# Layer 0's token routing: from a stage of its own into the last steps of the first attention

## What is computed

```python
xn = layernorm(x)
x  = x + attention(xn) + conditional(xn)
# conditional: 2 sequences of 1024 in the formula's default, here 8 of 256
s      = einsum("bnd,rd->brn", xn, routing_token)[:, 0]
a, b   = 0, -s
repeat 50 times:
    a  = log(k_eff) - logsumexp(s + b);  b = -relu(s + a)
scores = exp(s + a + b)
sel, idx = top_k(scores, num_tokens)      # 128 query tokens; 256 key tokens = all of them
light  = windowed attention over all tokens (8 heads)
heavy  = attention of the chosen tokens (8 heads) with a null key
out    = light + (heavy at idx, null_q elsewhere)
```

## Time and profile before

| | |
|---|---|
| median of 3 runs | 1793.24 us (1793.17, 1793.24, 1802.02) |
| the profiled execution | 1782.04 us, span 1780.20 us, mean granted TensorE clock 0.953 |
| busy: PE / DVE / ACT / POOL | 1575.2 / 1183.5 / 1002.4 / 375.5 us |
| first attention | 59.14 to 361.91 |
| routing stage | 361.91 to 384.14 |
| second attention | from 384.14 |

### The profile page before, as it was taken

The page is one execution under the profiler, slowest core; times in us unless marked ns, Lnnn a source line. Parts: engine busy times, 40 slices in busy tenths (PEclk is TensorE's granted clock), DMA queues, the critical chain, the costliest instruction groups (busy, mean ns, idle before and its releaser), DMA issues. The chain is left out here.

```text
span 1780.2 us, 31999 instructions
## 1 busy us (share of the span) xinstructions
PE 1575.2 (88%) x10960; PEld 1094.2 (61%) x10960; DVE 1183.5 (66%) x3106; ACT 1002.4 (56%) x2683; POOL 375.5 (21%) x386
## 2 busy tenths in 40 slices
PE   4799999959999999899999989588989957899986
PEld 2577777726666666567778766355556733555653
DVE  5599998747777777646545434577743358999964
ACT  2488887706666666444454434133453427888845
POOL 0100000000000000010122015332452410888830
PEclk8899999979999999989999999799999978999998
DMA  4000000040000000110000011400012130233200
GB/s 141 1 1 1 1 1 1 1 141 1 1 1 1 1 1 1 55 57 1 13 16 16 25 31 64 165 1 1 15 36 62 46 90 14 88 86 89 86 21 24
DMA packets 43980, 62.50 MB, mean 35 GB/s; under 512 B 7576, under 2 KB 29920, under 8 KB 43008
## 3 DMA queue, kind: packets, MB, share of 16 engines
q1 hardware_dynamic: 39280, 51.08, 9.6%
q0 software_dynamic: 4544, 9.38, 1.5%
HBM read 49.88 MB, written 15.75 MB: 37 GB/s over the span
## 5 line engine op out<-in xcount | busy, mean ns | idle before, releaser
L591 ACT ACTIVATE probs<-psum_all,pair_negmax 128x256 f32<-128x256 f32 x512 | 235.8, 473 | 158.9 <-DVE pair_negmax L690 86.7
L2116 POOL TENSOR_TENSOR weighted<-state,c_all 128x512 f32<-128x512 f32 x128 | 163.6, 1298 | 77.5 <-DVE state L2126 62.5
L690 DVE TENSOR_REDUCE pair_negmax<-psum_all 128x2 f32<-128x512 f32 x192 | 123.6, 685 | 66.9 <-PE psum_all L506 66.9
L2126 DVE TENSOR_TENSOR_SCAN state<-decay,psum_all 128x512 f32<-128x512 f32 x128 | 148.9, 1199 | 15.4 <-PE psum_all L2044 12.5
L716 DVE TENSOR_SCALAR probs<-probs,pair_recip 128x256 f32<-128x256 f32 x512 | 146.1, 349 | 4.5
L506 PE MATMUL psum_all<-keys,queryT 64*128 64x256 f32 x1024 | 143.9, 400 | 2.8 <-ACT probs L591 2.7
L602 ACT ACTIVATE probsT<-psum_all 128x512 f32<-128x512 f32 x256 | 140.0, 611 | 0.7 <-PE psum_all L517 0.5
L531 PE MATMUL psum_all<-probsT,values 128*64 128x256 f32 x1024 | 138.8, 392 | 0.0
L517 PE MATMUL psum_all<-ident,probs 128*128 128x128 f32 x1024 | 133.1, 273 | 2.8 <-ACT probsT L602 1.9
L517 PEld LDWEIGHTS psum_all<-ident,probs 128*128 128x128 f32 x1024 | 119.1, 141 | 18.1 <-issue 4.4
L506 PEld LDWEIGHTS psum_all<-keys,queryT 64*128 64x128 f32 x1024 | 92.6, 189 | 54.6 <-issue 46.6
(11 more groups left out here) (369 smaller groups left out, 3281.4 us busy)
## 6 DMA issues: line engine op xcount, KB each, us to landing
c_all<-c_rows SPq DMA_DIRECT2D x64, 256.0 KB, 3.3
slots<-slot_fill_dram SPq DMA_DIRECT2D x2, 2535.0 KB, 14.6
ring<-slots SPq DMA_DIRECT2D x18, 260.0 KB, 3.0
keys<-found SPq DMA_DIRECT2D x16, 256.0 KB, 4.7
up<-up_dram SPq DMA_DIRECT2D x1, 2048.0 KB, 7.8
down<-down_dram SPq DMA_DIRECT2D x1, 2048.0 KB, 12.3
up<-up_dram SPq DMA_DIRECT2D x1, 1408.0 KB, 6.1
found<-values,dest POOLq DMA_INDIRECT x78, 2.2
```

What stands on the lines that cost most here:

```text
L591: nc.scalar.activation(k.probs[:, 2 * (u % PAIR_BUF) + j, t, :], k.psum[score_bank(u, j)][:, SEQ * t:SEQ * (t + 1)], ACT.Exp, bias=k.pair_ ...
L690: nc.vector.reduce_max(k.pair_negmax[:, u % 2, SUB * j:SUB * (j + 1)], src, AXX, negate=True).then_inc(s.negmax_ready, 1)
L2116: nc.gpsimd.tensor_tensor(w.weighted[:, u % RING, :], w.state[:, u % RING, :], w.c_all[:, u // L3_DC % C_RING, :], ALU.mult)\
L2126: nc.vector.tensor_tensor_scan(w.state[:, u % RING, :], w.decay[:, u % L3_RING, :, :].rearrange("p b n -> p (b n)"), k.psum[u % PARTS_RING ...
```

## The change

`route_stage` goes, and with it one border between stages and the unread product of `keep_running` in it. Its operations move into the first attention:

- step 49: VectorE subtracts and clips the scores at its end, ScalarE makes the exponential; SP sends the scores and reads them back spread;
- step 50: VectorE makes the weights;
- step 51: the four transposes are a job of TensorE, `route_turn`, in bank 7 behind the values job of the last sequence, and VectorE saves it;
- steps 53 to 62: one rank pair at the end of each, on VectorE; steps 64, 65 and 66: two each;
- step 67: the choice, behind the last `add_output`.

The spread scores land in the upper half of `keys`, which the first attention doesn't use, since `probs` is in use there. Each rank pair now waits for the one before it, and all write the same two buffers; before, two pairs could be under way. The second attention gets the five new semaphores too but doesn't use them.

```diff
@@ -364,6 +364,8 @@
 PAIR_BUF, PAIR_TBUF = 3, 2
 PBUF = 4
 SEQS = BATCH
+ROUTE = Names(scores=DESCENT_STEPS + 1, exp=DESCENT_STEPS + 1, weights=DESCENT_STEPS + 2, turn=DESCENT_STEPS + 3,
+              ranks={DESCENT_STEPS + 5 + n: (n,) for n in range(10)} | {SEQS * PAIRS + i: (10 + 2 * i, 11 + 2 * i) for i in range(3)}, choice=SEQS * PAIRS + 3)
 
 
@@ -379,6 +381,8 @@
             (before if q == 0 else late[PAIRS * q - 5 + i]).append(job)
         if ffn:
             late[PAIRS * (q + 1) + 1].append(("null_probs", q, 0))
+    if not ffn:
+        late[ROUTE.turn].append(("route_turn", 0, 0))
     return before, early, late
 
...
-                 "output_made", "output_added", "route_dve", "route_act", "act_step", "dve_step") as s:
+                 "output_made", "output_added", "route_dve", "route_act", "act_step", "dve_step", "scored", "exped", "weighted", "sent", "spread") as s:
 
         def wait_saved(engine, job):
@@ -460,6 +464,12 @@
                     sp.dma_start(slots, k.dram["slot_fill"]).then_inc(s.filled, 16)
                 if fills:
                     sp.wait_ge(s.filled, 16 * len(fills))
+                if not ffn:
+                    sp.wait_ge(s.scored, 1)
+                    sp.dma_start(k.scratch, k.logits[0:BATCH, :]).then_inc(s.sent, 16)
+                    sp.wait_ge(s.sent, 16)
+                    sp.dma_start(c.w.scores_all[:, :, :].rearrange("p b n -> p (b n)"),
+                                 k.scratch.rearrange("b n -> (b n)").partition_broadcast(P)).then_inc(s.spread, 16)
 
             @block.tensor
@@ -485,6 +495,12 @@
                     elif what == "null_scores":
                         for t in range(SUB):
                             last = nc.tensor.matmul(jb[:, PAIRS * t:PAIRS * (t + 1)], xb[:, 1, P * t:P * (t + 1)], c.w.null_w[:, :], start=True, stop=True)
+                    elif what == "route_turn":
+                        pe.wait_ge(s.scored, 1)
+                        pe.wait_ge(s.weighted, 1)
+                        for a, rows in enumerate((k.logits, k.route_arg)):
+                            for t in range(SUB):
+                                last = nc.tensor.transpose(jb[:, 16 * (SUB * a + t):16 * (SUB * a + t + 1)], rows[:, P * t:P * (t + 1)], k.ident[0:16, 0:16])
                     elif what == "null_probs":
                         pe.wait_ge(s.null_weights, PAIRS // 2 * (q + 1))
@@ -624,6 +640,9 @@
                         save_out(u - V_AFTER)
                     if not ffn and u < DESCENT_STEPS:
                         descend(u)
+                    if not ffn and u == ROUTE.exp:
+                        act.wait_ge(s.scored, 1)
+                        nc.scalar.activation(k.route_exp[:, :], k.logits[:, :], ACT.Exp).then_inc(s.exped, 1)
                     for job in early[u] + late[u]:
                         do(job)
+                    elif what == "route_turn":
+                        ins = nc.vector.tensor_copy(k.route_cols[:, :, :, :].rearrange("p a t r -> p (a t r)"), jb[:, 0:4 * 16])
                     elif what == "values":
                         ins = nc.vector.tensor_copy(k.values[:, q % 2, :, 0:HD], jb[:, 0:SUB * HD].rearrange("p (t n) -> p t n", t=SUB))
@@ -745,83 +766,62 @@
                         normalise(u - 1)
                     for job in late[u]:
                         do(job)
-                    if not ffn and u <= DESCENT_STEPS:
...
+                    if ffn:
+                        continue
+                    if u <= DESCENT_STEPS:
                         descend(u)
-
-
-def route_stage(nc, k, w):
-
-
-    with signals(nc, "dve_step", "scored", "exped", "weighted", "sent", "spread", "turned", "cols_saved") as s:
-        with nc.Block() as block:
-            @block.vector
-            def _(dve):
-                step = Steps(dve, s.dve_step)
-                step.add(nc.vector.tensor_scalar(k.logits[:, :], k.logits[:, :], k.neg_a[:, :], 0.0, ALU.subtract, ALU.min))
-                step.wait()
-
-                nc.vector.tensor_scalar(k.logits[:, :], k.logits[:, :], -103.0, None, ALU.max).then_inc(s.scored, 1)
-                dve.wait_ge(s.exped, 1)
-                step.add(nc.vector.tensor_scalar(k.route_arg[:, :], k.route_exp[:, :], -1.0, 1.0, ALU.mult, ALU.add))
-                step.wait()
-                nc.vector.tensor_tensor(k.route_arg[:, :], k.route_arg[:, :], k.route_exp[:, :], ALU.add).then_inc(s.weighted, 1)
-                dve.wait_ge(s.turned, 1)
-
-                nc.vector.tensor_copy(k.route_cols[:, :, :, :].rearrange("p a t r -> p (a t r)"), k.psum[0][:, 0:4 * 16]).then_inc(s.cols_saved, 1)
-                dve.wait_ge(s.cols_saved, 1)
-                dve.wait_ge(s.spread, 16)
-                n = 0
-                for b in range(BATCH):
-                    for t in range(SUB):
-                        mine = k.route_cols[:, 0, t, b:b + 1]
-                        i = SUB * b + t
-                        if n >= 2:
-                            dve.wait_ge(s.dve_step, step.n - 2)
-                        step.add(nc.vector.tensor_scalar(w.compare[:, n % 2, :], w.scores_all[:, b, :], mine, 0.0, ALU.is_gt, ALU.add,
-                                                         accum_out=k.rank[:, 0, i:i + 1]))
-                        step.add(nc.vector.scalar_tensor_tensor(w.compare[:, 2 + n % 2, :], w.scores_all[:, b, :], mine, w.earlier[:, t, :],
-                                                                ALU.is_equal, ALU.mult, accum_out=k.rank[:, 1, i:i + 1]))
-                        n += 1
-                step.wait()
-                step.add(nc.vector.tensor_tensor(k.rank[:, 0, :], k.rank[:, 0, :], k.rank[:, 1, :], ALU.add))
-                step.wait()
-                selected = k.route_w[:, 0, :]
-                step.add(nc.vector.tensor_scalar(selected, k.rank[:, 0, :], float(NQ), None, ALU.is_lt))
-                step.add(nc.vector.tensor_scalar(k.route_w[:, 1, :], k.rank[:, 0, :], float(NQ), None, ALU.is_ge))
-                step.wait()
-                by_token = k.route_cols[:, 1, :, :].rearrange("p t r -> p r t")
-                step.add(nc.vector.tensor_tensor(selected.rearrange("p (b t) -> p b t", t=SUB), selected.rearrange("p (b t) -> p b t", t=SUB),
-                                                 by_token[:, 0:BATCH, :], ALU.mult))
-                step.add(nc.vector.tensor_copy(k.route_w[:, 2, :].rearrange("p (b t) -> p b t", t=SUB), by_token[:, BATCH:2 * BATCH, :]))
-
-            @block.scalar
-            def _(act):
-                act.wait_ge(s.scored, 1)
-                nc.scalar.activation(k.route_exp[:, :], k.logits[:, :], ACT.Exp).then_inc(s.exped, 1)
-
-            @block.sync
-            def _(sp):
-
-                sp.wait_ge(s.scored, 1)
-                sp.dma_start(k.scratch, k.logits[0:BATCH, :]).then_inc(s.sent, 16)
-                sp.wait_ge(s.sent, 16)
-                sp.dma_start(w.scores_all[:, :, :].rearrange("p b n -> p (b n)"),
-                             k.scratch.rearrange("b n -> (b n)").partition_broadcast(P)).then_inc(s.spread, 16)
-
-            @block.tensor
-            def _(pe):
-                pe.wait_ge(s.scored, 1)
-                for t in range(SUB):
-                    nc.tensor.transpose(k.psum[0][:, 16 * t:16 * (t + 1)], k.logits[:, P * t:P * (t + 1)], k.ident[0:16, 0:16])
-                pe.wait_ge(s.weighted, 1)
-                for t in range(SUB):
-                    last = nc.tensor.transpose(k.psum[0][:, 16 * (SUB + t):16 * (SUB + t + 1)], k.route_arg[:, P * t:P * (t + 1)],
-                                               k.ident[0:16, 0:16])
-                last.then_inc(s.turned, 1)
-                pe.wait_ge(s.dve_step, 2 + 2 * TILES - 14)
-                keep_running(nc, k, 7, 5)
-
-
+                    if u == ROUTE.scores:
+                        route_scores(nc, k, s, step)
+                    if u == ROUTE.weights:
+                        route_weights(nc, k, s, step)
+                    if u == DESCENT_STEPS + 5:
+                        wait_saved(dve, ("route_turn", 0, 0))
+                        dve.wait_ge(s.spread, 16)
+                    for m in ROUTE.ranks.get(u, ()):
+                        route_rank(nc, k, c.w, step, m)
+                    if u == ROUTE.choice:
+                        route_choice(nc, k, step)
+
+
+def route_scores(nc, k, s, step):
+
+    step.wait()
+    step.add(nc.vector.tensor_scalar(k.logits[:, :], k.logits[:, :], k.neg_a[:, :], 0.0, ALU.subtract, ALU.min))
+    step.wait()
+    nc.vector.tensor_scalar(k.logits[:, :], k.logits[:, :], -103.0, None, ALU.max).then_inc(s.scored, 1)
+
+
+def route_weights(nc, k, s, step):
+
+    nc.vector.wait_ge(s.exped, 1)
+    step.add(nc.vector.tensor_scalar(k.route_arg[:, :], k.route_exp[:, :], -1.0, 1.0, ALU.mult, ALU.add))
+    step.wait()
+    nc.vector.tensor_tensor(k.route_arg[:, :], k.route_arg[:, :], k.route_exp[:, :], ALU.add).then_inc(s.weighted, 1)
+
+
+def route_rank(nc, k, w, step, n):
+
```

(24 more changed lines are left out.)

2 lines of the change are left out of this document (1 added, 1 removed).

## The result

| | before | changed |
|---|---|---|
| median, 6 runs each | 1793.28 us (1789.81 to 1802.02) | 1778.05 us (1769.58 to 1780.15) |
| profiled execution, span | 1782.04, 1780.2 us | 1769.58, 1767.8 us |
| GpSimd opens the second attention | 384.14 | 363.64 |
| first scores of the second attention | 399.84 | 381.79 |

The ratio is 0.9911, with the interval [0.9890, 0.9932]: 15.2 us less by the medians, where 17.2 less and 1776.0 had been forecast.

What follows compares the result with a forecast made beforehand. The attention's steps were taken as bound by TensorE, the routing stage as a serial chain wholly on the path. Removing it gave -20.37 us net, the clock +3.2, so -17.2: 1776.0 us on the median's footing, range 1767 to 1784.

Steps and rivals of the forecast that it cites:

- next stage opens: GpSimd's first copy for the second attention was to come at 363.77 instead of 384.14, 20.37 us earlier.
- turn: End of step 51: TensorE waits for VectorE's save, then makes four transposes; +0.9 us, bounds 0.45 to 1.5.
- choice: Step 67, behind the last sum: VectorE's choice costs its own length, +0.68 us, bounds 0.5 and 1.0.
- border: The one stage border that stays, between the choice and GpSimd's first copy of the second attention: 0.28 us.
- steps 53 to 62: One rank pair of 0.81 us a step, hidden in VectorE's 1.13 us idle; 0.3 us stay, scores 4.46 us apart.
- opening: The second attention's opening was to run at granted clock 0.50 and last 18.5 us instead of 14.9.
- clock's term: Lower clock in the second attention's opening once the unread product is gone: +3.2 us, bounds 0 and +5.
- The part of the transfer: The spread scores' DMA takes 7.5 us; ranks ask for them 17.8 us later, so it was to cost nothing.
- VectorE as a new bound: Rival: ranks make VectorE the bound of steps 53 to 62, costing 2 to 8.1 us; 1778 to 1784; chance 0.12.
- a fall one job late: Second attention's opening: if the clock falls one job later than assumed, it costs about 2.6 us instead of +3.57.
- Given back later: Rival: later stretches lose 9 of the 17 us through openings falling otherwise on the clock; 1785; chance 0.10.
- ten further low steps: Rival: the second attention's first steps stay at 1.2 GHz, up to 4.46 us more each; 1820; chance 0.03.

Runs made afterwards that it cites:

- on A: The changed kernel repeated unaltered on chip A, against the kernel before on that chip: 1763.26 us, ratio 0.9900.
- on C: The changed kernel repeated unaltered on chip C, against the kernel before on that chip: 1767.93 us, ratio 0.9922.
- e6: The changed kernel with all 16 rank pairs in step 67 behind the last sum: 1792.52 us in one run, beside the kernel before's 1792.06.
- e5: The changed kernel with the turn one step later (52) and the choice one step earlier (66): 1760.53 us, ratio 0.9891 to the kernel before.
- e4: The changed kernel with two rank pairs in each of steps 53 to 60: 1784.34 us in one run, beside the kernel before's 1792.06.
- e2: The kernel before, with its routing stage but without the unread product at its end: 1783.59 us, ratio 1.0019 to the kernel before.
- e3: The changed kernel with unread bf16 products in the second attention's opening and at the first attention's end: 1757.46 us, ratio 0.9867 to the kernel before.
- e7: The changed kernel with e3 and e5 together, products in the first attention's opening and `keep_running` in the stage ahead: 1766.55 us, ratio 0.9845 to before.

## Why the prediction was right

By its own steps, the changed kernel's profile beside each:

| step | forecast | measured |
|---|---|---|
| next stage opens | 363.77 | 363.64, 363.83, 363.45, 365.01 |
| turn | +0.9 (0.45 to 1.5) | +0.80 |
| choice | +0.68 | 363.35 - 362.68 = +0.67 |
| border | 0.28 | 0.29 |
| steps 53 to 62 | 4.46 us, 0.3 us of cover | 4.46, 0.33 |
| opening | 18.5 instead of 14.9 | 17.35, 18.09, 16.89, 17.82; before 14.90, 16.84, 16.82, 17.03 |
| clock's term | +3.2 (0 to +5) | +2.45 in the first pair, +1.1 in the means |
| first copy, from step 51 | -20.37 | -20.5 |
| first scores | -17.2 | -18.05; means -18.7, from step 51 -19.4 |
| whole | -17.2, 1776.0 | -15.2, 1778.05; -17.9 on A, -11.9 on C |

- The mechanism of the removal held: one serial chain went from the path. Its largest part are the ranks, 13.03 us as they stood in it, and e6 shows that they come back on the path when they are not covered. The part of the transfer was hidden: nothing stalls at step 53. Counted from step 51, -20.5 us at GpSimd's first copy against -20.37 is the prediction's best hit, and it repeats.
- The turn is right in total and split a little otherwise: the wait 0.45, as forecast, the transposes 0.35 for four, 0.09 each. e5 shows that the wait was a matter of the step chosen.
- VectorE as a new bound did not come. e4 shows that the rival's mechanism exists and where it starts: with a second pair a step. The forecast's condition, 0.3 us of cover, was the right thing to look at.
- The clock's term was the weakest. The mechanism held in the main (low clock in nearly the whole opening; without the product, before pays too, e2). Mis-sized was the baseline: I read one opening of before, and it was the shortest of four. Also, the clock did not fall between the attentions in any of the four profiles of the changed kernel: their first pair jobs take 2.05, 2.79, 1.98 and 2.53 us, where a low one takes 2.92. The working had priced that case, a fall one job late, at about 2.6, against +2.45 measured over the first profile, and took 3.2; the opening of 18.5 us among its signs goes with 3.57, not with 3.2. By the Trainium skill (TensorE: Matmul & The Clock Gate, What's actually happening) throttled is the default and activity releases it; the fall in the opening agrees (0.55 over 363.64 to 382.00), as does e3, in which more activity held 1.00. That the opening starts low, which the prediction drew from it, did not come in these four.
- "Given back later" stood at 0.10, as a case in which most of the gain goes. That did not come. In the three repeats without "remote" waits 2.4 of 18.5 us are gone by the end in the mean, which is not clear of chance, and in the first profile 9.0 us go with those waits.
- The 1776.0 is in part luck. It adds 11 us to the profile's sum because the runs of before lay so far above its profile; for the changed kernel that distance is 8.5 us (1778.05 - 1769.58), and nothing shows what makes it. Profile against profile the first pair gives -12.5, the timed runs -15.2, -17.9 and -11.9, and the forecast -17.2 lies among them. Less was lost in the opening than the 3.2 us forecast, and perhaps some us later that the sum had at nothing.
- One slip in a rival changes nothing here: ten further low steps would be +27 us, which is 1.5% and not 0.5%; six give 0.5%. The clock rises within 382 to 390, as in the forecast, and the rival did not come.

What stays open: whether the profile of before would show "remote" waits at the time when it took 1792 us, and whether the 2.4 us are more than chance. The timed ratios (0.9911, 0.9900, 0.9922) agree within their intervals, so the gain does not hang on either.

## What to carry to other kernels

A stage that one engine walks through as a serial chain is worth its whole length if its pieces fit into idle time that recurs elsewhere; read that idle time per step, ahead of the instruction that ends it, and fill it to just under its size (one pair of 0.81 in 1.13 us cost nothing, two cost 0.5 us a step once the slack between the engines was used up, here after three steps). Put a moved TensorE job into a step in which nothing it must wait for has just been issued. Where work leaves TensorE thin ahead of an opening, look at the granted clock of several executions before pricing it, and try unread products in the gaps: here they were worth 5.8 us, more than the finer placing of turn and choice (1.1). To compare timelines of two executions, count from an instruction just ahead of the change, not from the start of the span.

## What the runs showed of the hardware

- An opening of dependent TensorE jobs with gaps of 0.78 to 0.85 us loses the clock: 14.9 to 18.2 us, and 12.13 us with products in the gaps, at 1.00. The products in the gaps don't lengthen it; five at the end of the stage ahead cost 0.6 us in e7.
- The clock's fall lies elsewhere in each execution of one kernel: openings from 14.90 to 17.03 us with the same instructions.
- One chip ran the kernel before in 1792 us and some minutes later in 1780 and 1784. At the first time profiles of three variants of the changed kernel show waits of 2 to 7 us with no releaser on the core ("remote"), most of them at the same few lines of two attentions; one profile of before there later, and eight on two other chips, show none.
- An accumulating pair on 128 x 256 takes 0.81 us when its instructions follow freely and 0.93 us when each pair waits for the last.
